# A graph network's gate pass: all gates in PSUM, a step's gates made in two pieces

## The reference

```python
att = jax.nn.sigmoid(xs @ W_att[:d] + xd @ W_att[d:] + b_att)   # xs = x[src], xd = x[dst]
messages = (xs @ W_msg + b_msg) * att
aggregated = jax.ops.segment_sum(messages, dst, num_segments=num_nodes)
```

## Time and profile before

| | us |
|---|---|
| median of 3 runs (4019.29 to 4022.37) | 4019.59 |
| the profiled execution | 4025.97 |
| its span | 4024.1 |
| gate pass in it, from the first gates to the last sum | 1202 to 1638 |

### The profile page before, as it was taken

How to read it: one execution, slowest core, us unless ns; L and a number is a source line. 1 busy time by engine, 2 the same in 40 slices (tenths; PEclk the granted TensorE clock), 3 DMA queues, 4 the chain that set the end, 5 groups by cost and what they waited for, 6 DMA issues and landing times. The chain is left out here.

```text
span 4024.1 us, 70549 instructions
## 1 busy us (share of the span) xinstructions
PE 3172.9 (79%) x23417; PEld 2267.1 (56%) x23529; DVE 2350.8 (58%) x7900; ACT 1236.7 (31%) x2830; POOL 2715.7 (67%) x2717
## 2 busy tenths in 40 slices
PE   4887888888778888745544449987999889997996
PEld 3766666666656666423322235546666666675554
DVE  6888888998747777666766752243333433333223
ACT  3333344455435555344322330003111211112112
POOL 4777777777517777467657657736777577774774
PEclk7899999999889999855555579998999999998998
DMA  5434445567735555043335379946999589996995
GB/s 156 117 83 107 106 112 114 132 136 143 183 89 141 142 139 143 18 97 72 75 85 113 76 186 295 292 148 215 305 306 300 193 285 302 304 301 201 296 294 184
DMA packets 529216, 702.83 MB, mean 175 GB/s; under 512 B 72345, under 2 KB 420648, under 8 KB 528084
## 3 DMA queue, kind: packets, MB, share of 16 engines
q1 hardware_dynamic: 421204, 436.31, 38.3%
q0 software_dynamic: 107648, 261.94, 23.7%
HBM read 579.27 MB, written 118.69 MB: 173 GB/s over the span
## 5 line engine op out<-in xcount | busy, mean ns | idle before, releaser
L1749 POOL DMA_INDIRECT pass_rows<-table_sage,src_idx x1040 | 994.8, 957 | 353.0 <-issue 298.0
L1132 POOL DMA_INDIRECT first_rows<-table_tensor,src_idx x772 | 770.5, 998 | 246.7 <-issue 231.9
L1798 PE MATMUL pass_dense_ps<-x 128*128 128x512 f16 x3528 | 602.6, 327 | 31.7 <-DMA x<-table_sage 29.5
L2855 POOL DMA_INDIRECT sort_rows<-table_sort,slot_idx x392 | 400.2, 1021 | 170.9 <-issue 158.5
L1798 PE MATMUL pass_dense_ps<-rb 128*128 128x512 f16 x2646 | 468.4, 332 | 25.9 <-DMA rb<-table_sage 21.4
L1798 PEld LDWEIGHTS pass_dense_ps<-x 128*128 128x128 bf16 x3528 | 335.0, 98 | 244.3 <-DMA x<-table_sage 31.6
L1386 POOL DMA_INDIRECT pass_rows<-table_gate,src_idx x314 | 335.1, 1067 | 134.2 <-issue 93.6
L1798 PEld LDWEIGHTS pass_dense_ps<-rb 128*128 128x128 bf16 x2646 | 229.5, 98 | 233.5 <-DMA rb<-table_sage 21.1
L1877 DVE TENSOR_TENSOR pass_scaled_sums<-pass_sums_ps,rc 128x52 f32<-128x52 f32 (+16 forms) x316 | 56.9, 222 | 515.8 <-PE pass_sums_ps L1840 462.4
L1219 PE MATMUL pass_sums_ps<-pass_hot,pass_prod_a 128*128 128x128 f32 x1568 | 234.8, 296 | 151.4 <-DVE rb L1236 136.3
L1219 PEld LDWEIGHTS pass_sums_ps<-pass_hot,pass_prod_a 128*128 128x128 f32 x1568 | 202.3, 201 | 208.5 <-DVE rb L1236 184.1
(11 more groups left out here) (387 smaller groups left out, 6354.8 us busy)
## 6 DMA issues: line engine op xcount, KB each, us to landing
rb<-dense SPq DMA_DIRECT2D x196, 288.0 KB
x<-dense SPq DMA_DIRECT2D x294, 192.0 KB
x<-table_sage SPq DMA_DIRECT2D x294, 192.0 KB
rb<-dense SPq DMA_DIRECT2D x98, 309.5 KB
pass_counts<-dense SPq DMA_DIRECT2D x147, 192.0 KB
rb<-table_sage SPq DMA_DIRECT2D x294, 96.0 KB
dense<-re SPq DMA_DIRECT2D x49, 448.0 KB
dense<-x SPq DMA_DIRECT2D x42, 448.0 KB, 5.8
```

Source lines behind the costliest of these rows:

```text
L1132: nc.gpsimd.indirect_dma_start(rows[:, h, t, :], None, table, bass.IndirectOffsetOnAxis(ap=idx[:, at:at + 1], axis=0)).then_inc(gathered[h ...
L1749: nc.gpsimd.indirect_dma_start(rows[:, h, t, :], None, table, bass.IndirectOffsetOnAxis(ap=idx[:, at:at + 1], axis=0)).then_inc(gathered[h ...
L1798: ins = nc.tensor.matmul(dense_ps[:, a * bank_cols + at:a * bank_cols + to], table_ring[:, k, from_table:from_table + P], counts_ring[:, k ...
L2855: nc.gpsimd.indirect_dma_start(rows[:, b, j, :], None, table, bass.IndirectOffsetOnAxis(ap=slot_idx[:, at:at + 1], axis=0)).then_inc(gathe ...
```

## The change

`gates_apart` is gone. `gate_ps` is three banks (1536 columns): even steps have columns 0 to 767, odd steps 768 to 1535. So the middle bank (512 to 1023) is shared: its first half belongs to even steps, its second to odd ones. A step's gates are made by two instructions on ACT: first the 512 columns that lie in the step's own bank, then the 256 in the shared bank. Ahead of the second there is a new wait, `weighed` n, so that DVE has finished with the gates of step n-1 before anything is written to the bank that they share. `gates_made` is signalled by the second. Nothing else differs: DVE's and PE's instructions, the DMAs and the order of all other work are the same.

```diff
-        weighted, gates_apart = s.sb("weighted", [P, 2, SUPER_COLS]), s.sb("gates_apart", [P, SUPER_COLS])
+        weighted = s.sb("weighted", [P, 2, SUPER_COLS])
...
-        dense_ps, gate_ps = s.ps("dense", [P, 1024]), s.ps("gate", [P, 1024])
+        dense_ps, gate_ps = s.ps("dense", [P, 1024]), s.ps("gate", [P, 2 * SUPER_COLS])
...
         def gates_of(n):
-            return gate_ps[:, 0:SUPER_COLS] if n % 2 == 0 else gates_apart[:]
+            return gate_ps[:, n % 2 * SUPER_COLS:(n % 2 + 1) * SUPER_COLS]
...
                 if n >= 2:
                     act.wait_ge(weighed, n - 1)
                 act.wait_ge(streamed[k], 32 * (n // GATE_STREAM + 1))
-                nc.scalar.activation(gates_of(n), at_dense[:], ACT.Sigmoid,
+                alone, shared = ((0, 512), (512, SUPER_COLS)) if n % 2 == 0 else ((1024 - SUPER_COLS, SUPER_COLS), (0, 1024 - SUPER_COLS))
+                nc.scalar.activation(gates_of(n)[:, alone[0]:alone[1]], at_dense[:, alone[0]:alone[1]], ACT.Sigmoid,
+                                     bias=messages[:, k, P:width])
+                if n >= 1:
+                    act.wait_ge(weighed, n)
+                nc.scalar.activation(gates_of(n)[:, shared[0]:shared[1]], at_dense[:, shared[0]:shared[1]], ACT.Sigmoid,
                                      bias=messages[:, k, P:width]).then_inc(gates_made, 1)
```

## The result

The changed kernel is slower. Its median is 4051.82 us (4045.62 to 4054.32, 4 runs) beside 4019.44 for the kernel before (4017.67 to 4022.37, 4 runs), a ratio of 1.0073 with a 95% interval of 1.006 to 1.0086: 24 to 35 us. The profiled execution took 4045.62 us with a span of 4043.7. Forecast were 4038.0 us, 18.4 us more, and a range of 4015 to 4053. Sign and cause were right. The size was a third too small: 18.4 us against 29 by the ratio. The median lies near the upper end of the range, and 0.8 us above the narrower one of 4028 to 4051 that the sum had for its own case.

What follows compares the result with a forecast made beforehand. POOL's gathers were taken to bound the gate pass; afterwards DVE would: 365.8 + 68.9 plus unfilled waits gives 445.9 us against 427.5, +18.4 on the median, 4038.0 us. Range 4015 to 4053.

Steps and rivals of the forecast that it cites:

- the sum: Gate pass: DVE's own walk 365.8 us, plus 68.9, plus waits that can't be filled: 445.9 us, +18.4; chance 0.71.
- POOL is the pace before the change: Gate pass: POOL's unbroken file of gathers sets the pace, 5.4 us a group against 4.7 for DVE's own walk.
- the stretch: Gate pass on DVE, first to last multiplication of hot_sig: 427.5 us before, forecast 446 us after.
- Part 1: Odd steps' gates leave SBUF: gathers no longer delayed by SBUF weighs, POOL's file 21.5 us shorter, gain not collected.
- Part 2: Shared-bank wait: second weigh 1.57 us after first, L1585 at 2.44, with own rows 2.93; adds 68.9 us to DVE.
- From the stretch to the kernel: Gate pass's +18.4 us put on the 4019.59 median, 6.4 below the profiled execution of 4025.97: kernel 4038.0 us.
- POOL's relief collected: Rival: consumers keep up with POOL's shorter file, gate pass loses up to 21.5 us; 3998 us; chance 0.08.
- The delay swallowed by waits: Rival: waits already in DVE's gate pass absorb the delay, time the same, 4020 to 4027 us; chance 0.16.
- The compounding case: Rival: PE's clock falls in the gate pass, or DVE finds sums late; 6.2 us a group, 4077 us; chance 0.05.

Runs made afterwards that it cites:

- no_shared: Changed kernel with odd steps' gates in a PSUM bank of their own, no added wait, some gates left out (wrong); stretch 406.5 us, ratio 0.9948 to before.
- before_reads_early: Kernel before, with DVE's register reads of start positions moved right after a group's first weigh; stretch 420.4 us, ratio 0.9992 to before.
- wait_only: Kernel before, odd gates still in SBUF, with gates made in two instructions and the unneeded added wait; stretch 453.0 us, ratio 1.0059 to before.
- split_only: Kernel before, with each step's gates made in two ACT instructions and no added wait; stretch 427.8 us, ratio 1.0003 to before.
- reads_early: Changed kernel, with DVE's register reads of start positions moved right after a group's first weigh; stretch 419.0 us, ratio 0.9987 to before.
- weigh_pieces: Changed kernel, with DVE's weigh in two instructions, shared columns first, and ACT's second piece waiting for those only; stretch 424.5 us, ratio 0.9990 to before.
- hybrid: Kernel before, with odd steps' gates 512 columns in their own PSUM bank, 256 in SBUF, no wait; stretch 409.9 and 406.4 us, ratios 0.9955 and 0.9951.

## Why the prediction was right, and where its size was off

- **POOL is the pace before the change.** Shown: taking 20.3 us off its gathers took 21.0 us off the stretch (no_shared), and taking the register reads, 23.8 us of idle time, out of DVE's walk took only 7.1 off it (before_reads_early), of which 5.5 stand against shorter gathers.
- **Part 1, a relief of 21.5 us for POOL that isn't collected.** The gathers lost 25.1 us in the changed kernel and 20.3 in no_shared. (One reading was off by a little: the 314 gathers together are 38.4 us over 945 ns each, not 37.9.) That it is worth nothing beside the wait is shown by wait_only: 453.0 us with the relief and without it.
- **Part 2, 1.57, 2.44 and 2.93 us.** Measured 1.55, 2.42 and 2.94 as medians over all groups with two steps. With these the term comes to 68.8 us, and 68.9 held. That ACT's second instruction lies in its idle time is shown by split_only.
- **The sum, 445.9 us.** It was 453.0, 7.1 more, in two terms. First, DVE's own walk was taken over as it stood, 365.8 us; but the register reads ahead of the sums took 28.4 us under issue and not 23.8. In some groups of the kernel before hot_sig was ready when the last weigh ended, L1585 followed at once, and a part of the reads was over before L1585 ended, presumably done while the weigh was running. Now hot_sig comes last. Of the groups numbered from 0, the gap ahead of the sums went from nothing to 1.13 us in group 53, from 0.83 to 1.44 in group 69, and in group 61 from 0.90 to 1.42 (the first line is from before the change, the second from after):

```profile
1544.28 0.23 DVE L1596 TENSOR_TENSOR ra<-ra,pass_sums_ps 128x76 f32 x1 [0.90 <-issue]
...
1561.78 0.23 DVE L1601 TENSOR_TENSOR ra<-ra,pass_sums_ps 128x76 f32 x1 [1.42 <-issue]
```

Over all groups these gaps grew by 5.0 us. That this is the reason for the growth is argued from the order of the instructions; that the reads are in DVE's walk is shown by reads_early. Second, some 2 us of waits for PE stayed that I had let the longer walk fill, in groups 1 and 59 above all (1.61 and 0.97 us).
- **From the stretch to the kernel.** The 25.4 us of the stretch and the 28 to 29 by the ratios agree within the intervals. The step from one profiled execution to the median was weaker than it looks. The forecast took 6.4 us off, as the median before lay that much below its profiled execution; after the change it lies 6.2 above it. And the profiled execution itself rose by 19.7 us, close to the 18.4 forecast, but that is luck: the stretch rose by 25.4 and the rest of the execution happened to be 5.8 shorter (3596.6 and 3590.8 us). Over all the profiles that rest scatters from 3590.8 to 3613.5.
- **The rivals.** POOL's relief collected: not in this kernel, but no_shared shows that the price, 21.5 us, was right, and the condition too: DVE's walk has to stay under POOL's. The delay swallowed by waits: it took 0.73 us a group or less, and it was 1.00; weigh_pieces, which brings it down, is the case (424.5 us). The compounding case: the granted clock was 0.95 in the stretch before and after, so nothing of it happened. In the experiments it lay between 0.93 and 0.99 and doesn't order the stretches: 0.93 with 427.8 us (split_only), 0.95 with 427.5 (before) and with 453.0 (after), 0.96 and 0.97 with 406.4 and 409.9 (hybrid).

## What to carry to other kernels

Where a bank or buffer is shared so that a second one can move, count the loop that its wait closes: here ACT's 0.48 us of work and the two hand-overs went into DVE's order in 69 groups, and what ACT does behind the waiting instruction went in too. What others wait for should stand ahead of a waiting instruction in its engine's queue (16 us here), and the consumer should hand back the shared part first (27 us). And ask of every relief which engine will be the pace once it is there: a relief of 20 us gave 21 where POOL stayed the pace, and one of 16 or 25 gave nothing where DVE was.

## What the runs showed of the hardware

- A gather that begins while DVE runs an instruction with both inputs in SBUF is held up till that is over: of 51 gathers begun inside weighs out of SBUF 48 were long, and the held ones end 0.82 us after the weigh does; of 44 begun inside weighs out of PSUM none was (947 ns at most). One that is already under way when such a weigh begins isn't held up (26 of them, 957 ns at most). With all weighs reading one input from PSUM, gathers of over 1.15 us fell from 74 to 29 of 314, and the mean from 1067 to 987 ns.
- Reading start positions into DVE's registers, up to nine for one group, stands in DVE's way for 1.1 to 1.5 us where nothing covers it (1.9 the first time). It appears only as idle time under issue. Moved to where DVE waits anyway, it took 33 us off a pass of 452.
- The wait for ACT's second piece, 0.60 us in the median of 70 groups, is booked under issue in 59 of them and under ACT in 9. The timeline tells what it is: the weigh starts 0.09 us after the piece's end.
